# Column groups of TensorE for the sum over keys and for three conditioning vectors

## The chip, the cores and the metric

The kernel runs on one core of a Trainium2 chip. The metric is the device time of the whole program in microseconds (us), lower is better. Before the change it was 969.02 us, the median of three runs that lay between 968.61 and 970.26.

The core has five engines that run their own instruction streams and wait for each other through semaphores. PE (TensorE) multiplies matrices: it takes a stationary operand (loaded by a separate record, PEld) and streams a moving one through it into PSUM. DVE (VectorE) and ACT (ScalarE) do elementwise work, POOL (GpSimd) issues the indirect transfers here, SP issues nearly all others.

## The reference

One transformer block on X of shape (4, 512, 512), with a conditioning vector c of shape (4, 512). All is float32. Cut to what matters:

```python
mod = (silu(c) @ wmod).reshape(4, 6, 1, 512)          # six conditioning vectors per batch
sa, ca, ga, sb, cb, gb = mod[:, 0], ..., mod[:, 5]
ga, gb = away_from_zero(ga), away_from_zero(gb)       # sign * max(|.|, 0.25)
h = layernorm(x) * (1 + ca) + sa
# linear attention
Q, K, V = split(h @ W_in.T + b_in)
Q, K = rope(Q), rope(K)
A = sum over the 512 keys of (K / |K|) * V            # one row of 512 per batch
x = x + ga * ((A * Q) @ W_out.T + b_out + h)
# mixture of experts: 64 experts, 8 per token, and a shared one
h = layernorm(x) * (1 + cb) + sb
x = x + gb * moe(h)
```

The sum A is the operation in question. Per batch it is a product of a vector of 512 weights (1/|K| of each key) with a matrix of 512 keys by 512 features (K * V).

## The kernel before, in words

Tokens lie on the 128 partitions. A batch is 512 tokens, so it has TPB = 4 tiles of 128, and a row of 512 features has KC = 4 chunks of 128. The front part of the program (up to about 370 us of the profile) computes attention, the gate scores and the shared expert, batch by batch; then tiles of tokens, sorted by expert, go through the 64 experts (L1656 to L1676), and at the end the eight results of each token are read back and added.

The order is written out by hand, engine by engine. On PE (function under `@block.tensor`, from L1380) a batch goes: keys and values for each tile (`keys_values`, L1434), queries (`queries`, L1445) with the sum over keys between the second and third chunk (`sum_keys`, L1456) and `turn_sums` (L1468) behind the third, then `project` (L1479). For batch 0 the sum stands between the third and the fourth chunk of queries. Within `sum_keys` four products follow each other, one per tile of 128 keys: stationary is one column of `krn` (128 keys x 1), moving the tile of `kv` (128 keys x 512 features), and all four add into one row of PSUM bank 7. DVE copies this row into `arow` (`take_sums`, L1002), and `turn_sums` turns it into four columns with four products of one partition by 128 against a 1 (`ones1`). DVE then takes the columns (L1011) and weighs W_out with them (`weigh_w_out`, L1015), for which `project` waits.

The conditioning vectors come from `modulate(m)` (L1391): four products each, stationary four columns of silu(c), moving 128 x 512 of `wmod`, into a bank of its own. Vectors 0 to 2 are made at the start, 3 to 5 behind the keys and values of batch 0. DVE takes vectors 3 to 5 in `away_from_zero(5, ...)` (L933 to L937) and L1204, L1205, and then signals `s_modr`; PE waits for it ahead of the sum of batch 0 (the bank of vector 4 is the one the sum writes). DVE does this behind the key work, `residual(0)` and `stats1(1)`.

Each product in float32 is two records of PE in the trace, each with its own load of the stationary operand: four products are "x8", the twelve of vectors 3 to 5 "x24".

POOL scatters the places of the chosen tokens into a table (L583, 32 transfers per batch), starting when DVE has the places of a batch (L1025), and later gathers tokens (L621) for the expert phase.

Of the kernel before, what the change touches and what calls it, by code (L numbers as in the profile page):

```python
# [27 lines left out]
P = 128  # L28
BATCH = 4
SEQ = 512  # L30
D = 512
# [58 lines left out]
def build(nc, x_in, w_in, b_col, b_row, w_out, b_out, gates, experts, c_t, w_mod, tables, rope_rows,  # L90
# [8 lines left out]
    with ctx:  # L99
# [42 lines left out]
        ones_bf = sb("ones_bf", [P, P], BF16)  # L142
        ones1 = sb("ones1", [P, 1])
        tbl = sb("tbl", [P, DUMMY_COL + 1], I32)
        pair = sb("pair", [P, TILES, TOPK], I32)
# [40 lines left out]
        place = [sb(f"place{i}", [P, TPB, TOPK], I32) for i in range(2)]  # L186
        arow = region[5][0:1, 0:D]
        count_f = sb("count_f", [EV, 1])
# [40 lines left out]
        sum_bank = [bank[i] for i in (0, 1, 2, 3, 6)]  # L229
        mod_bank = [bank[m][0:BATCH, :] for m in (0, 1, 4, 6, 7, 0)]  # L230

# [25 lines left out]
        s_silu = sem("s_silu")  # L257
        s_mod = sem("s_mod")
        s_modv = sem("s_modv")
        s_modT = sem("s_modT")  # L260
# [598 lines left out]
        def _(ve):  # L859
# [5 lines left out]
            ve.memset(ones_bf[:, :], 1.0).then_inc(s_cst, 1)  # L865
            ve.memset(ones1[:, :], 1.0).then_inc(s_cst, 1)
            ve.memset(mask[:, :, 0:1], 1.0).then_inc(s_cst, 1)
            ve.memset(seen[:, TPB, :], 0.0).then_inc(s_cst, 1)
# [60 lines left out]
            def away_from_zero(m, to):  # L929

                g = mod_bank[m]
                ve.wait_ge(s_mod, m + 1)
                t0.mark(ve.tensor_scalar(mod_t[0], g, 0.0, 2.0, ALU.is_ge, ALU.mult))  # L933
                step(t0, ve.tensor_scalar(mod_t[2], g, -1.0, 0.25, ALU.mult, ALU.max))
                step(t0, ve.tensor_tensor(mod_t[1], g, mod_t[2], ALU.max))
                step(t0, ve.tensor_scalar(mod_t[2], mod_t[0], -1.0, None, ALU.add))
                step(t0, ve.tensor_tensor(to, mod_t[2], mod_t[1], ALU.mult))  # L937
# [33 lines left out]
            def key_roots(b):  # L971
# [3 lines left out]
                if b:  # L975
                    ve.wait_ge(s_rn, b)
                    ve.wait_ge(s_ar, b)
                one_over_root(t, 2, krn[:, :], s_rn)
# [18 lines left out]
            def take_sums(b):  # L997

                ve.wait_ge(s_ar, b + 1)
                if b:  # L1000
                    ve.wait_ge(s_as, b)
                ve.tensor_copy(arow[:, :], bank[7][0:1, :]).then_inc(s_arow, 1)  # L1002

# [198 lines left out]
            stats1(1)  # L1202
            away_from_zero(5, modr[1][:, 2, :])
            t0.mark(ve.tensor_scalar(modr[1][:, 0, :], mod_bank[4], 1.0, None, ALU.add))  # L1204
            step(t0, ve.tensor_copy(modr[1][:, 1, :], mod_bank[3]))  # L1205
# [175 lines left out]
        def _(pe):  # L1381
# [3 lines left out]
            def modulate(m):  # L1385
# [7 lines left out]
                mm.then_inc(s_mod, 1)  # L1393

            modulate(0)
            modulate(1)
# [52 lines left out]
            def sum_keys(b):  # L1449
# [5 lines left out]
                for i in range(TPB):  # L1455
                    mm = pe.matmul(bank[7][0:1, :], krn[:, i:i + 1], kv[:, i, :], start=(i == 0), stop=(i == TPB - 1))  # L1456
                mm.then_inc(s_ar, 1)

            def turn_sums(b):

                pe.wait_ge(s_arow, b + 1)
                pe.wait_ge(s_cst, 2)
                if b:
# [3 lines left out]
                for c in range(KC):  # L1467
                    mm = pe.matmul(bank[6][:, c:c + 1], arow[:, c * P:(c + 1) * P], ones1[0:1, :], start=True, stop=True)  # L1468
                mm.then_inc(s_as, 1)
# [109 lines left out]
            keys_values(0, *[(i, j) for i in range(TPB) for j in range(2)][1:])  # L1579
            for m in range(3, NMOD):  # L1580
                modulate(m)
            pe.wait_ge(s_modr, 1)
# [13 lines left out]
            pe.wait_ge(s_late, 16 * 4)  # L1596
            pe.wait_ge(s_cst, 5)
            for b in range(BATCH):
# [201 lines left out]
```

## Time and profile before

| | |
|---|---|
| time, median of 3 | 969.02 us (968.61 to 970.26) |
| span of the profiled execution | 1061.7 us |
| PE busy in it | 944.7 us (89%) |
| DVE busy | 547.2 us (52%) |
| POOL busy | 479.2 us (45%) |
| mean granted clock of PE | 0.960 |

The profile is one execution, and its span is the only time shown for it: it is 92.7 us above the median of the timed runs. The granted clock is a share of the full 2.4 GHz; in the windows of the trace it is 1.00 or 0.50, and values between are stretches with both.

In the rows below, a timeline line reads: start in us, busy us, engine, source line, operation, what is written and read, shape, how many, and in brackets the idle time of the engine before it with what ended it. A "x8" line merges eight records that follow each other; the last record of a group overlaps the next group's start. Chain lines read: start, us, what.

### The profile page before, as it was taken

The numbers are of one execution on the slowest core, as the hardware profiler recorded it, in microseconds if no ns is written. First come the engines' busy times: TensorE is split into PE (matmuls) and PEld (weight loads), VectorE is DVE, ScalarE is ACT, GpSimd is POOL, SyncE is SP. The second block draws the span as 40 slices with busy tenths as digits, with TensorE's granted clock in tenths as the row PEclk, the third lists the DMA queues.
The fourth block names the chain that finished last, engine by engine and source line by source line (L and its number), as shares of the span: only waits on it lengthen the run. The fifth ranks groups of instructions, "written<-read, shape, count | busy, mean of one in ns | idle before, by whom it ended". The sixth has DMA issues, their size and how long they took to land.

```text
span 1061.7 us, 18602 instructions
## 1 busy us (share of the span) xinstructions
PE 944.7 (89%) x3569; PEld 571.9 (54%) x3570; DVE 547.2 (52%) x1460; ACT 263.6 (25%) x789; POOL 479.2 (45%) x468
## 2 busy tenths in 40 slices
PE   7999999999995688989998889989898999887697
PEld 2434544544534246766766666667575666665243
DVE  4676776687685443433433334343434334343888
ACT  2122222222212103323323323233332233232000
POOL 0000066045266664555565555556565655555500
PEclk9999999999996898999999999999999999999699
DMA  9922021003021424666566666666567665797697
GB/s 345 330 69 75 1 67 28 40 1 95 0 62 43 136 80 148 222 201 216 199 193 208 241 225 212 229 199 227 197 222 227 207 213 196 250 403 263 230 420 312
DMA packets 68518, 192.06 MB, mean 181 GB/s; under 512 B 19926, under 2 KB 20438, under 8 KB 68104
## 3 DMA queue, kind: packets, MB, share of 16 engines
q1 hardware_dynamic: 38232, 120.28, 32.6%
q0 software_dynamic: 30256, 71.43, 20.5%
q8 instruction: 12, 0.20, 0.1%
q14 instruction: 18, 0.15, 0.0%
HBM read 158.98 MB, written 52.54 MB: 199 GB/s over the span
## 4 chain that ended last, share of the span: by engine, by line
PE 66%; another core or an unknown queue 8%; issue 7%; DVE 5%; DMA 4%; DVEq 1%; ACT 1%; ACTq 1%; POOLq 0%; POOL 0%; SPq 0%
PE bank L1661 19%; PE bank L1669 11%; PE bank L1434 7%; PE bank L1656 6%; PE bank L1479 5%; PE bank L1730 4%; PE bank L1445 4%; PE bank L1543 3%; PE bank L1676 2%; DMA front<-y_rows 2%; PE bank L1562 2%; DMA front<-h_rows,gid 1%; DVE front L1297 1%; PE bank L1456 1%
## 5 line engine op out<-in xcount | busy, mean ns | idle before, releaser
L1661 PE MATMUL bank<-wqkv,h2T 128*128 x1280 | 310.7, 387 | 0.0
L631 POOL DMA_INDIRECT y_rows<-front,sid x160 | 164.7, 1030 | 202.7 <-issue 90.7
L1661 PEld LDWEIGHTS bank<-wqkv,h2T 128*128 128x128 f32 x1280 | 236.6, 195 | 26.7
L583 POOL DMA_INDIRECT slot_table<-pair,place x128 | 131.1, 1024 | 249.6 <-DVE place L1025 186.5
L621 POOL DMA_INDIRECT front<-h_rows,gid x167 | 172.1, 1030 | 68.5 <-issue 46.0
L1311 DVE COPY front<-bank 128x128 f32<-128x128 f32 x160 | 46.6, 291 | 268.4 <-remote 154.4
L1669 PE MATMUL bank<-wqkv,front 128*128 x320 | 171.3, 618 | 1.3 <-DVE front L1311 1.3
L817 ACT ACTIVATE h2T<-bank 128x512 f32<-128x512 f32 x162 | 96.5, 596 | 245.8 <-PE bank L1656 145.4
L1656 PEld LDWEIGHTS bank<-const,front 128*128 128x128 f32 x648 | 82.1, 144 | 100.4 <-issue 97.2
L1305 DVE COPY front<-bank 128x512 f32<-128x512 f32 x160 | 110.0, 688 | 40.7 <-PE bank L1669 28.8
L1434 PE MATMUL bank<-wqkv,front 128*128 128x512 f32 x256 | 117.3, 610 | 8.3 <-DVEq L957 6.2
L1656 PE MATMUL bank<-const,front 128*128 128x128 f32 x648 | 100.7, 280 | 11.4 <-DMA front<-h_rows,gid 5.8
L1676 PE MATMUL bank<-const,front 128*128 128x128 f32 x160 | 45.7, 286 | 51.4 <-DVE front L1297 51.2
L1434 PEld LDWEIGHTS bank<-wqkv,front 128*128 128x128 f32 x256 | 48.5, 195 | 67.7 <-issue 58.8
L823 ACT ACTIVATE front<-bank 128x128 f32<-128x128 f32 x160 | 43.6, 272 | 98.8 <-PE bank L1661 76.3
L1297 DVE SCALAR_TENSOR_TENSOR front<-bank,wgt,front 128x128 f32<-128x128 f32 x160 | 56.0, 350 | 19.9 <-ACT front L823 16.4
L1479 PE MATMUL bank<-front 128*128 128x512 f32 x128 | 58.4, 609 | 2.9 <-DVE front L1015 2.1
L1676 PEld LDWEIGHTS bank<-const,front 128*128 128x128 f32 x160 | 22.7, 142 | 68.9 <-DVE front L1297 49.3
L1445 PE MATMUL bank<-front,wqkv 128*128 128x512 f32 x128 | 57.6, 599 | 0.0
L1669 PEld LDWEIGHTS bank<-wqkv,front 128*128 128x128 f32 x320 | 48.7, 192 | 14.7 <-issue 3.8
L1730 PE MATMUL bank<-front,const 128*128 128x512 f32 x92 | 45.1, 641 | 9.3 <-DMA front<-y_rows 9.3
L832 ACT ACTIVATE wgt<-front 128x1 f32 x160 | 32.5, 203 | 72.3 <-issue 45.4
(247 smaller groups left out, 775.2 us busy)
## 6 DMA issues: line engine op xcount, KB each, us to landing
wqkv<-in_experts SPq DMA_DIRECT2D x64, 768.0 KB
front<-y_rows SPq DMA_DIRECT2D x20, 768.0 KB, 9.3
wqkv<-y_rows SPq DMA_DIRECT2D x12, 768.0 KB, 11.7
front<-in_w_mod SPq DMA_DIRECT2D x5, 1024.0 KB, 10.5
x<-in_x SPq DMA_DIRECT2D x4, 1024.0 KB, 11.2
h_rows<-h SPq DMA_DIRECT2D x4, 1024.0 KB
out_dram<-x SPq DMA_DIRECT2D x16, 256.0 KB, 7.8
wqkv<-in_w_in SPq DMA_DIRECT2D x3, 1024.0 KB, 13.6
```

Of the source, the lines that this page charges most:

```text
L583: pool.indirect_dma_start(out=slots[:, :], out_offset=bass.IndirectOffsetOnAxis(ap=place[b % 2][:, i, k:k + 1], axis=0), in_=pair[:, b * T ...
L621: pool.indirect_dma_start(out=xg[s], out_offset=None, in_=h2_rows[:, :], in_offset=bass.IndirectOffsetOnAxis(ap=gid[:, s:s + 1], axis=0), ...
L631: pool.indirect_dma_start(out=y_rows[:, :], out_offset=bass.IndirectOffsetOnAxis(ap=sid[:, s:s + 1], axis=0), in_=yb[s % YBUFS], in_offset ...
L817: sc.activation(h2T[:, s % 4, :], bank[s % 2][:, :], ACT.Copy).then_inc(s_xT, 1)
L1305: ve.tensor_copy(yb[s % YBUFS], bank[4 + s % 2][:, :]).then_inc(s_y, 1)
L1434: mm = pe.matmul(bank[2 + j][:, :], hT[:, k, i * P:(i + 1) * P], win[:, k, (j + 1) * D:(j + 2) * D], start=(k == 0), stop=(k == KC - 1))
L1445: mm = pe.matmul(bank[4 + c % 2][:, :], win[:, k, c * P:(c + 1) * P], hT[:, k, :], start=(k == 0), stop=(k == KC - 1))
L1479: mm = pe.matmul(bank[4 + i % 2][:, :], qT[:, k, i * P:(i + 1) * P], woa[:, k, :], start=(k == 0), stop=(k == KC - 1))
L1656: mm = pe.transpose(bank[s % 2][:, k * P:(k + 1) * P], xg[s][:, k * P:(k + 1) * P], ident)
L1661: mm = pe.matmul(bank[2 + s % 2][:, 0:GU], xT[s % 4][:, k, :], wqkv[:, bass.ds(w + k * GU, GU)], start=(k == 0), stop=(k == KC - 1))
L1669: pe.matmul(bank[4 + s % 2][:, :], iT[s % 2], wqkv[:, bass.ds(w + KC * GU, D)], start=True, stop=True).then_inc(s_d, 1)
L1676: pe.transpose(bank[6 + s % 2][:, 0:P], inter[s % 2], ident).then_inc(s_I, 1)
```

## The change

The four products of the sum go to four different groups of 32 columns of the array (`tile_position=(0, 32 i)`), each with the column of `krn` repeated 32 times, so that each writes 32 equal rows of bank 7; none adds to another. DVE copies all 128 rows. `turn_sums` now multiplies the 128 partitions with a vector `heads` that is 1 at partitions 0, 32, 64 and 96 and 0 elsewhere, which adds the four partial sums. `heads` is made by five small memsets on DVE at the start. `s_ar` counts four per batch.

Vectors 3 to 5 are written to three column groups of bank 6 (partitions 64, 32 and 0), and the loops are exchanged: for each of the four chunks the three vectors follow each other. PE waits for all three pieces of `wmod` ahead of the first product, and DVE waits for all three vectors. Line numbers after the change are some 20 higher: L1456 becomes L1478, L1468 L1491, L1391 of vectors 3 to 5 L1411.

```diff
-        arow = region[5][0:1, 0:D]
+        arow = region[5][:, 0:D]
...
+        QUAD = P // TPB
+        mod_bank = [bank[m][0:BATCH, :] for m in (0, 1, 4)] + [bank[6][q * QUAD:q * QUAD + BATCH, :] for q in (2, 1, 0)]
...
+            step(t0, ve.memset(heads[:, :], 0.0))
+            for i in range(TPB):
+                ve.memset(heads[i * QUAD:i * QUAD + 1, :], 1.0).then_inc(s_cst, 1)
...
-                ve.tensor_copy(arow[:, :], bank[7][0:1, :]).then_inc(s_arow, 1)
+                ve.tensor_copy(arow[:, :], bank[7][:, :]).then_inc(s_arow, 1)
...
+            def modulate_side_by_side(ms):
+                for m in ms:
+                    pe.wait_ge(s_wmod[m], 16)
+                for k in range(KC):
+                    for m in ms:
+                        q = (NMOD - 1 - m) * QUAD
+                        mm = pe.matmul(mod_bank[m], silu_c[:, k * BATCH:(k + 1) * BATCH], wmod[m][:, k, :],
+                                       start=(k == 0), stop=(k == KC - 1), tile_position=(0, q))
+                        if k == KC - 1:
+                            mm.then_inc(s_mod_late, 1)
...
                 for i in range(TPB):
-                    mm = pe.matmul(bank[7][0:1, :], krn[:, i:i + 1], kv[:, i, :], start=(i == 0), stop=(i == TPB - 1))
-                mm.then_inc(s_ar, 1)
+                    at = slice(i * QUAD, (i + 1) * QUAD)
+                    mm = pe.matmul(bank[7][at, :], krn[:, i:i + 1].to_broadcast([P, QUAD]), kv[:, i, :], start=True, stop=True,
+                                   tile_position=(0, i * QUAD))
+                    mm.then_inc(s_ar, 1)
...
-                    mm = pe.matmul(bank[6][:, c:c + 1], arow[:, c * P:(c + 1) * P], ones1[0:1, :], start=True, stop=True)
+                    mm = pe.matmul(bank[6][:, c:c + 1], arow[:, c * P:(c + 1) * P], heads[:, :], start=True, stop=True)
```

On PE, batch 0, from vector 3 to `turn_sums`, the kernel before has this order, with the semaphores each instruction waits for (`front` holds `wmod`, `kv`, `hT` and `arow`):

```order
32 L1391 MATMUL bank<-front,silu_c 4x512 [waits s_wmod3]
33 L1391 MATMUL bank<-front,silu_c 4x512 x3
34 L1391 MATMUL bank<-front,silu_c 4x512 [waits s_wmod4]
35 L1391 MATMUL bank<-front,silu_c 4x512 x3
36 L1391 MATMUL bank<-front,silu_c 4x512 [waits s_wmod5]
37 L1391 MATMUL bank<-front,silu_c 4x512 x3
38 L1445 MATMUL bank<-front,wqkv 128x512 [waits s_win_q,s_modr]
```

The changed kernel at the same place:

```order
32 L1411 MATMUL bank<-front,silu_c 4x512 [waits s_wmod5,s_wmod4,s_wmod3]
33 L1411 MATMUL bank<-front,silu_c 4x512 x11
34 L1466 MATMUL bank<-front,wqkv 128x512 [waits s_win_q,s_modr]
35 L1466 MATMUL bank<-front,wqkv 128x512 x7
36 L1466 MATMUL bank<-front,wqkv 128x512 [waits s_qT]
37 L1466 MATMUL bank<-front,wqkv 128x512 x3
38 L1478 MATMUL bank<-front,krn 32x512 [waits s_kvp,s_rn,s_modr]
39 L1478 MATMUL bank<-front,krn 32x512 x3
```

There are still twelve products for the vectors and four for the sum, at the same places among the others; only the order among the twelve and the three waits have moved. The wait for `s_modr` ahead of the sum stands where it stood.

## Rows read from the trace of the kernel before

**Rows 1.** The page: shares of the chain that ended last, by engine.

```profile
PE 66%; another core or an unknown queue 8%; issue 7%; DVE 5%; DMA 4%; DVEq 1%; ACT 1%; ACTq 1%; POOLq 0%; POOL 0%; SPq 0%
```

**Rows 2.** The timeline of PE, batch 0, from vector 3 to the first projection.

```profile
49.69 10.46 PE L1391 MATMUL bank<-front,silu_c 128*4 128x512 f32 x24
60.08 10.57 PE L1445 MATMUL bank<-front,wqkv 128*128 128x512 f32 x24
70.58 3.59 PE L1456 MATMUL bank<-front,krn 128*1 128x512 f32 x8
74.10 3.70 PE L1445 MATMUL bank<-front,wqkv 128*128 128x512 f32 x8
...
78.26 1.03 PE L1468 MATMUL bank<-ones,front 1*128 1x1 f32 x8
...
82.41 5.37 PE L1479 MATMUL bank<-front 128*128 128x512 f32 x8 [2.10 <-DVE front L1015]
```

**Rows 3.** Line L1456 (ns min/median/max), and the groups of 0 to 345 us (L1445: busy us, mean ns).

```profile
L1456 PEld LDWEIGHTS bank<-front,krn x32: 79/84/84, 70.6 to 299.6; 128*1 128x1 f32 x32
L1456 PE MATMUL bank<-front,krn x32: 590/592/592, 70.6 to 300.0; 128*1 128x512 f32 x32
...
L1445 PEld LDWEIGHTS bank<-front,wqkv 128*128 128x128 f32 x128 | 23.7, 190 | 31.1 <-issue 31.1
```

**Rows 4.** The timeline of DVE in the same stretch of batch 0.

```profile
69.23 0.67 DVE L1205 COPY h2T<-bank 4x512 f32<-4x512 f32 x1
...
73.38 0.69 DVE L994 TENSOR_TENSOR front<-front 128x512 f32<-128x512 f32 x1
74.21 0.68 DVE L1002 COPY front<-bank 1x512 f32<-1x512 f32 x1
...
79.32 0.16 DVE L1011 COPY asum<-bank 128x4 f32<-128x4 f32 x1 [0.70 <-PE bank L1468]
```

**Rows 5.** Windows: stretch, busy us (and count) per engine, clock, DMA share, GB/s.

```profile
49.69:60.10 10.41, 10.41 (x26) 2.02 (x25) 9.23 (x23) 0.00 (x0) 0.00 (x0) 1.00 0.35 128
60.10:70.58 10.48, 10.48 (x26) 4.46 (x25) 9.65 (x30) 1.37 (x2) 0.00 (x0) 1.00 0.00 0
```

**Rows 6.** The loads of `wmod`: the timeline of SP, and line L402.

```profile
33.58 2.72 SPq L402 DMA_DIRECT2D front<-in_w_mod  x3
...
DMA to landing us min/median/max: 8.0/10.5/14.5
```

**Rows 7.** The chain that ended last, the sums of batches 1 and 3.

```profile
141.36 3.52 PE bank L1456 x8
...
297.05 3.52 PE bank L1456 x8
```

**Rows 8.** The timeline of DVE and PE in batch 1.

```profile
145.99 0.67 DVE L1002 COPY front<-bank 1x512 f32<-1x512 f32 x1
...
148.45 1.05 PE L1468 MATMUL bank<-ones,front 1*128 1x1 f32 x8
```

**Rows 9.** Windows behind three waits of PE, columns as in rows 5.

```profile
82.41:85.90 3.49, 3.49 (x5) 1.42 (x6) 0.00 (x0) 0.00 (x0) 0.00 (x0) 0.51 0.74 205
...
370.10:376.00 5.90, 5.86 (x10) 2.20 (x11) 2.24 (x9) 0.60 (x1) 0.78 (x1) 0.50 0.42 137
...
344.00:348.70 4.70, 4.70 (x9) 2.09 (x10) 4.06 (x14) 2.44 (x6) 3.48 (x5) 0.50 0.04 6
```

**Rows 10.** The timeline of PE behind another wait, and behind a long one.

```profile
127.04 3.70 PE L1434 MATMUL bank<-wqkv,front 128*128 128x512 f32 x8 [2.16 <-DVEq L957]
...
344.00 0.21 PE L1573 MATMUL bank<-mask,tri_bf 128*128 128x65 bf16 x1 [5.76 <-issue]
```

**Rows 11.** The timeline of POOL, first and last scatter of one unbroken row.

```profile
290.30 0.97 POOL L583 DMA_INDIRECT slot_table<-pair,place  x1 [19.38 <-DVE place L1025]
...
366.62 0.96 POOL L583 DMA_INDIRECT slot_table<-pair,place  x1 [0.30 <-issue]
```

**Rows 12.** The waits, 300 to 400 us: who waited for whom, us, times, longest.

```profile
DVE cum L1268 <- remote: 11.8, 1, 11.8
```

More of the change, by code:

```diff
@@ L143, in build @@
         ones1 = sb("ones1", [P, 1])
+        heads = sb("heads", [P, 1])
         tbl = sb("tbl", [P, DUMMY_COL + 1], I32)
@@ L229, in build @@
         sum_bank = [bank[i] for i in (0, 1, 2, 3, 6)]
-        mod_bank = [bank[m][0:BATCH, :] for m in (0, 1, 4, 6, 7, 0)]
+        QUAD = P // TPB
+        mod_bank = [bank[m][0:BATCH, :] for m in (0, 1, 4)] + [bank[6][q * QUAD:q * QUAD + BATCH, :] for q in (2, 1, 0)]
         s_const = sem("s_const")
@@ L258, in build @@
         s_mod = sem("s_mod")
+        s_mod_late = sem("s_mod_late")
         s_modv = sem("s_modv")
@@ L931, in away_from_zero @@
                 g = mod_bank[m]
-                ve.wait_ge(s_mod, m + 1)
+                if m >= 3:
+                    ve.wait_ge(s_mod_late, 3)
+                else:
+                    ve.wait_ge(s_mod, m + 1)
                 t0.mark(ve.tensor_scalar(mod_t[0], g, 0.0, 2.0, ALU.is_ge, ALU.mult))
@@ L976, in key_roots @@
                     ve.wait_ge(s_rn, b)
-                    ve.wait_ge(s_ar, b)
+                    ve.wait_ge(s_ar, TPB * b)
                 one_over_root(t, 2, krn[:, :], s_rn)
@@ L997, in take_sums @@
             def take_sums(b):
-                ve.wait_ge(s_ar, b + 1)
+                ve.wait_ge(s_ar, TPB * (b + 1))
                 if b:
                     ve.wait_ge(s_as, b)
-                ve.tensor_copy(arow[:, :], bank[7][0:1, :]).then_inc(s_arow, 1)
+                ve.tensor_copy(arow[:, :], bank[7][:, :]).then_inc(s_arow, 1)
             def weigh_w_out(b):
@@ L1203, in _ @@
             away_from_zero(5, modr[1][:, 2, :])
+            ve.wait_ge(s_mod_late, 3)
             t0.mark(ve.tensor_scalar(modr[1][:, 0, :], mod_bank[4], 1.0, None, ALU.add))
@@ L1455, in sum_keys @@
                 for i in range(TPB):
-                    mm = pe.matmul(bank[7][0:1, :], krn[:, i:i + 1], kv[:, i, :], start=(i == 0), stop=(i == TPB - 1))
-                mm.then_inc(s_ar, 1)
+                    at = slice(i * QUAD, (i + 1) * QUAD)
+                    mm = pe.matmul(bank[7][at, :], krn[:, i:i + 1].to_broadcast([P, QUAD]), kv[:, i, :], start=True, stop=True,
+                                   tile_position=(0, i * QUAD))
+                    mm.then_inc(s_ar, 1)
             def turn_sums(b):
                 pe.wait_ge(s_arow, b + 1)
-                pe.wait_ge(s_cst, 2)
+                pe.wait_ge(s_cst, 2 + TPB)
                 if b:
@@ L1579, in _ @@
             keys_values(0, *[(i, j) for i in range(TPB) for j in range(2)][1:])
-            for m in range(3, NMOD):
-                modulate(m)
+            modulate_side_by_side(range(3, NMOD))
             pe.wait_ge(s_modr, 1)
@@ L1596, in _ @@
             pe.wait_ge(s_late, 16 * 4)
-            pe.wait_ge(s_cst, 5)
+            pe.wait_ge(s_cst, 5 + TPB)
             for b in range(BATCH):
```

## The prediction

> **What bounds the kernel now.** I read the page first, then the chain, then the timelines of PE and DVE around each sum, then the windows for the clock. PE carries 66% of the chain [rows 1]; in the front part the sums of batches 1 to 3 stand on the chain, each with 3.52 us [rows 7]. So PE time removed there is at first sight time removed from the kernel. Batch 0 is different. PE makes vectors 3 to 5 from 49.69, the queries from 60.08, and starts the sum at 70.58 [rows 2]. The sum must wait for DVE's signal behind L1205, which ends at 69.23 + 0.67 = 69.90 [rows 4]. DVE is busy 9.23 of the 10.41 us and 9.65 of the 10.48 us ahead of it [rows 5], with work (keys, residual, statistics) that doesn't need vectors 3 to 5 until its very end. So PE has only about 0.5 us of slack there: DVE bounds that place nearly as much as PE does.
>
> The profiled span is 1061.7 us and the median 969.02, a gap of 92.7 us. The chain holds 8% (some 85 us) of "another core or an unknown queue", on a program with one core [rows 1]. My estimate is that these pauses come with being profiled. The changed places lie early, where the rows show none, so I take the differences worked out inside the profile one for one off 969.02.
>
> **The products themselves.** Thirty-two records for sixteen products: each product is two passes, 0.592 us long each, but one starts every 3.52 / 8 = 0.44 us [rows 2, 3, 7]. A product's two passes use the same columns, so they can't lie on top of each other. If PE starts its records in program order, the first pass of the next product starts only when the second pass of this one has started. Then what overlaps is always a second pass with the next product's first. Four products take 5 steps in place of 8: 5 x 0.43 + 0.08 = 2.2 us, against 3.52. The twelve products of the vectors take 13 steps in place of 24, 5.6 us in place of 10.3, a saving of 4.7.
>
> No row shows a column group, so the crossing into and out of the groups is bounded. Below: nothing, since records of different shapes already follow each other unbroken, the sum ends 3.52 us after its start and the queries start at 74.10 [rows 2]. Above: the array empties twice, 2 x (0.592 - 0.43) = 0.32 us, and one small weight load of 0.08 and one of 0.19 are uncovered [rows 3]: 0.6 us. I take 0.3, the middle. By the Trainium skill (TensorEngine Tiling (Array Packing), Key Properties) a change of tiling mode drains TensorE, which speaks against the change; by it the sum would be nearer to the upper end, about 1 us less gain over the four sums.
>
> So a sum gains 3.52 - 2.2 - 0.3 = 1.0 us.
>
> **Batch 0.** The vectors are made 4.7 - 0.3 = 4.4 us earlier and the queries with them, but then PE reaches the sum at about 66 and waits for DVE until about 70.0, with the sum, the last queries and `turn_sums` queued behind. Of the 4.4 us, 0.5 is gain. If the cover were gone, all 4.4 would count. The wait for all three loads at once costs nothing: issued by 33.58 + 2.72 = 36.3, they land at most 14.5 us later [rows 6], by about 50.8, and the queries queued behind would at most start a microsecond later: up to 4 us of delay would hide in the new wait. With the sum's 1.0 batch 0 stands at 1.5.
>
> The new wait of about 4 us has a price: the clock. Behind the 2.10 us wait at 82.41 PE ran at 0.51 for 3.49 us, 1.2 in place of 2.4 GHz, and eight records took 5.37 us [rows 2, 9]; behind one of 5.76 us it was at 0.50 for 4.70 us, and in another place for 5.90 us [rows 9, 10]. Behind a wait of 2.16 us nothing fell (3.70 us for eight) [rows 10]. A wait of 4 us I take to be long enough; the loss is then half the stretch, 1.7 us for the shortest row (up to 2.9 for the longest), and the work from 70.0 to `turn_sums` is all on the path, because DVE waits 0.70 us for `turn_sums` ahead of L1011 [rows 4]. On the other hand the 1.7 us lost at 82.41 was luck of place, as the pair of rows shows, and I give 4 in 10 that it doesn't come again: 0.7 back. Batch 0 in sum: 1.5 - 1.7 + 0.7 = 0.5 us.
>
> **Batches 1 and 2.** PE comes from work without a wait into the sum and goes on with queries. `turn_sums` needs `arow`, and DVE copies it at 145.99 to 146.66, directly behind its rotation of the queries, not because it waits for the sum [rows 8]. `turn_sums` starts at 148.45: 1.7 us is the most that any faster sum can give there. 1.0 is below it. Two batches: 2.0 us.
>
> **Batch 3.** The same 1.0 us on PE. But POOL scatters without a real pause from 290.30 to 367.6, and this row starts from the places of batch 2, ahead of the sum at 297.05 [rows 7, 11]. In the profile DVE comes later still, at 368.9, after 11.8 us in one of those foreign pauses [rows 12]; if unprofiled runs lack it, POOL is what the gathers wait for, and batch 3's gain vanishes. I count half, 0.5 us.
>
> **The rest.** Five memsets on DVE at the start lie under its wait for x; the copy of 128 rows in place of one takes the time of other 128 x 512 operations, 0.69 against 0.67 to 0.68 [rows 4]. `turn_sums` reads 128 partitions in place of one; bounds: 1.03 us for its eight records now, at most 8 x 0.02 more; nothing taken. The loads of 32 columns in place of one lie under the passes.
>
> Sum: 0.5 + 2.0 + 0.5 = 3.0 us, so 969.0 - 3.0 = **966.0 us**. Its own range, with the crossing at 0 to 0.6, the clock loss in batch 0 at 0 to 2.9 and batch 3 at 0 to 1.3, is 963.8 to 968.5.
>
> **Rival 1: all four groups run at once.** Then a sum takes two passes, 0.9 us, and with the crossing 1.2: a gain of 2.3, capped at 1.7 in batches 1 to 3 by DVE's copy. Batch 0: 0.5 + 2.3 - 1.7 + 0.7 = 1.8. With half of batch 3: 1.8 + 3.4 + 0.85 = 6.0, so 963.0 us. For it: nothing in the rows forbids a queue that holds the second passes back and lets later first passes go. Against it: the even spacing of 0.44 us that two passes of one product show. The Trainium skill (TensorE: Matmul & The Clock Gate, Part 3: Packing small matmuls) reports three column groups at 2.38 times the speed, for single-pass products, and says that matmuls start and end strictly in program order. By its ratio alone this rival would be right; by its ordering, my forecast is. Chance 0.22.
>
> **Rival 2, slower: no overlap, and the crossing is paid.** If two float32 passes in different column groups don't run together, every sum keeps its 3.5 us and gets 0.6 on top: 4 x 0.6 = 2.4 us, plus 0.1 where the vectors' own 0.6 exceeds the slack of 0.5 in batch 0: 971.5 us. It decides from 0.5 us per crossing on, where four of them pass 0.2%. For it: the trace has no pair of PE records that overlap by more than the 0.16 us of an ending pass. Against: the groups write different partitions and hold different weights. Chance 0.15.
>
> **Rival 3: the gain is given back.** Sums shorter by 1.0 us, but the clock in batch 0 stays low for 4.7 to 5.9 us as in the longer rows, the fall at 82.41 comes too, and batch 3 is swallowed: 1.5 - 2.6 + 2.0 = 0.9 us, 968.1 us. Chance 0.13.
>
> **How the numbers follow.** My forecast has the remaining 0.50. About 0.2% (1.9 us) is what a measurement of this kernel tells from no change, so faster means below 967.1 and slower above 971.0. Faster: 0.7 of my case, nearly all of rival 1: 0.35 + 0.21 = 0.56. Slower: most of rival 2 and a remnant of mine, 0.14. The rest, 0.30, is no change. The range reaches from rival 1 with a smaller crossing (961.8) to the lower part of rival 2 (970.8).
>
> **What the profile after would show.** L1478 "x8" spanning 2.2 to 2.5 us in batches 1 to 3 with starts in overlapping pairs (my case), about 1.0 to 1.2 (rival 1), or 3.6 and more (rival 2). L1411 "x24" at about 6 us, then a wait of about 4 us ahead of L1478 that ends with DVE's L1205 counterpart at about 70, and a clock of 0.5 behind it. `turn_sums` of batch 1 about 1 us nearer to the end of DVE's copy. I would be wrong if the new wait left the clock at 1.00, if the crossings were over 1 us, or if the later waits of about 2 us, whose clock falls in one place and not in another, all changed sides together: four of them at 1.7 us each weigh more than the change.

## The result and the profile after

The changed kernel takes 968.75 us (median of 20 runs, 964.20 to 971.22). The kernel before, in 20 runs beside it, takes 972.10 (968.61 to 974.26). The ratio is 0.9971, with a 95% interval of 0.9961 to 0.9982: faster by 0.29%, some 2.8 us. (The two medians differ by 3.35 us.) The forecast was 3.0 us less than before. Its time, 966.0 us, lies 2.75 us below the measured one: the three runs that it started from (median 969.02) were low ones of their kind, and 20 runs have 972.10.

The difference came out near the forecast, but not by its reasons: that it is near is luck. The sums became faster than forecast by more than a factor of two, falls of the clock took much of that back, and the two errors nearly cancel.

Shares of the chain that ended last, from the page of the kernel after:

```profile
PE 64%; DMA 9%; POOL 6%; DVE 5%; issue 5%; SPq 1%; DVEq 1%; ACT 0%; POOLq 0%
```

The entry for another core or an unknown queue [rows 1] is gone, and the span is 966.1 us against 968.06 timed for the same execution. POOL has come in with 6%: the row of scatters.

PE in batch 0, after:

```profile
50.93 3.61 PE L1411 MATMUL bank<-front,silu_c 128*4 128x512 f32 x24
54.47 10.57 PE L1466 MATMUL bank<-front,wqkv 128*128 128x512 f32 x24
71.19 1.93 PE L1478 MATMUL bank<-front,krn 128*32 128x512 f32 x8 [6.16 <-DVEq L1216]
73.06 4.32 PE L1466 MATMUL bank<-front,wqkv 128*128 128x512 f32 x8
...
77.90 1.05 PE L1491 MATMUL bank<-heads,front 128*128 128x1 f32 x8
...
82.07 6.61 PE L1502 MATMUL bank<-front 128*128 128x512 f32 x8 [2.19 <-DVE front L1024]
```

Against [rows 2]: the vectors take 54.47 - 50.93 = 3.54 us in place of 10.39. PE then stands for 6.16 us, until DVE has taken the vectors, and the sum behind this wait takes 1.87 us, as much as two passes at half clock. The eight records behind the next wait take 6.61 us, not 5.37.

The last of the vectors on DVE, and its copy of the sum:

```profile
70.40 0.69 DVE L1215 COPY h2T<-bank 4x512 f32<-4x512 f32 x1
...
75.28 0.69 DVE L1011 COPY front<-bank 128x512 f32<-128x512 f32 x1
```

It ends at 71.09, within 0.1 us of PE's restart: DVE decides that start. The copy of 128 rows takes what the one of a single row took [rows 4].

Windows behind the two waits (us, busy time and count of PE, PEld, DVE, ACT and POOL, granted clock, DMA share, GB/s):

```profile
71.00:74.50 3.50, 3.31 (x10) 1.03 (x11) 3.22 (x6) 0.00 (x0) 0.00 (x0) 0.52 0.09 22
82.00:88.00 6.00, 5.93 (x7) 2.52 (x8) 0.00 (x0) 0.00 (x0) 0.00 (x0) 0.50 0.79 279
```

The granted clock is half, 1.2 GHz in place of 2.4. Before, PE ran through the first place without a wait, and the second stretch was shorter [rows 9].

The sum of batch 1, and how its passes lie, in the timeline and in two windows that cut it at the middle:

```profile
143.91 1.06 PE L1478 MATMUL bank<-front,krn 128*32 128x512 f32 x8
144.91 0.70 PE L1466 MATMUL bank<-front,wqkv 128*128 128x512 f32 x1
```

```profile
143.91:144.34 0.43, 0.43 (x5) 0.15 (x8) 0.14 (x1) 0.32 (x1) 0.27 (x1) 1.00 0.00 0
144.34:144.91 0.57, 0.57 (x9) 0.01 (x1) 0.17 (x1) 0.36 (x1) 0.57 (x1) 1.00 0.04 1
```

The sum takes 144.91 - 143.91 = 1.00 us; before it was 3.52 [rows 7]. In the first window PE has five records: the end of a query's, and four of the sum. So four passes run at once, and the other four begin about 0.45 us after the first; the second window counts all eight and the next query.

What ends the way to `turn_sums` there now, from the chain (start, us, what):

```profile
144.02 0.70 ACT front L722
...
144.74 0.69 DVE front L996
145.43 0.65 DVE front L997
...
148.73 0.61 DVE front L1011
...
149.38 1.05 PE bank L1491 x8
```

The sum has left the chain. ACT's turn of the queries and DVE's rotation stand in its place, and PE waits for the copy in each of the batches 1 to 3:

```profile
149.38 1.05 PE L1491 MATMUL bank<-heads,front 128*128 128x1 f32 x8 [0.78 <-DVE front L1011]
...
232.06 1.05 PE L1491 MATMUL bank<-heads,front 128*128 128x1 f32 x8 [0.75 <-DVE front L1011]
...
299.65 1.05 PE L1491 MATMUL bank<-heads,front 128*128 128x1 f32 x8 [0.76 <-DVE front L1011]
```

POOL, first scatter from the places of batch 2, last scatter ahead of the gathers, first gather:

```profile
287.52 0.96 POOL L586 DMA_INDIRECT slot_table<-pair,place  x1 [18.84 <-DVE place L1034]
...
364.04 0.97 POOL L586 DMA_INDIRECT slot_table<-pair,place  x1 [0.30 <-issue]
365.31 1.05 POOL L624 DMA_INDIRECT front<-h_rows,gid  x1 [0.30 <-issue]
```

The gather follows the scatters without a pause, so POOL ends the front part. The longer idle times in this row (6.04 us once, 1.46 us three times) end with transfers of its own table, none with PE or DVE: what batch 3 gains in its sum lies beside it. From the first gather to the end it is 600.8 us here.

### The profile page after: what moved, and what is told of

It is laid out like the page before. It is cut to its first block, busy times and chain, and to the rows that moved or that the text cites. A ratio compares the mean times of both kernels' runs of the same rounds, so it can differ in the third digit from the quotient of the medians.

```text
span 966.1 us, 18609 instructions
## 1 busy us (share of the span) xinstructions
PE 902.5 (93%) x3569; PEld 560.6 (58%) x3570; DVE 553.5 (57%) x1465; ACT 271.1 (28%) x789; POOL 478.2 (49%) x468
## 4 chain that ended last, share of the span: by engine, by line
PE 64%; DMA 9%; POOL 6%; DVE 5%; issue 5%; SPq 1%; DVEq 1%; ACT 0%; POOLq 0%
PE bank L1683 25%; PE bank L1691 13%; PE bank L1455 7%; PE bank L1678 6%; POOL slot_table L586 5%; PE bank L1502 5%; DMA wqkv<-in_experts 3%; PE bank L1752 3%; PE bank L1466 2%; PE bank L1698 2%; DMA front<-y_rows 1%; DMA wqkv<-y_rows 1%; DMA front<-h_rows,gid 1%; DMA slot_table<-pair,place 1%; PE bank L1566 1%
## 5 line engine op out<-in xcount | busy, mean ns | idle before, releaser
L1683 PE MATMUL bank<-wqkv,h2T 128*128 x1280 | 303.1, 380 | 0.3 <-DMA wqkv<-in_experts 0.3
L1683 PEld LDWEIGHTS bank<-wqkv,h2T 128*128 128x128 f32 x1280 | 230.7, 190 | 25.4 <-issue 0.6
L1691 PE MATMUL bank<-wqkv,front 128*128 x320 | 164.2, 595 | 1.6 <-DVE front L1321 1.5
L1678 PEld LDWEIGHTS bank<-const,front 128*128 128x128 f32 x648 | 80.3, 141 | 92.9 <-issue 83.1
L1678 PE MATMUL bank<-const,front 128*128 128x128 f32 x648 | 97.5, 273 | 7.3 <-DMA front<-h_rows,gid 6.5
L1198 DVE TENSOR_SCALAR gid<-tbl 128x1 int32 x167 | 25.7, 154 | 82.3 <-issue 69.0
L1752 PE MATMUL bank<-front,const 128*128 128x512 f32 x92 | 43.1, 618 | 10.0 <-DMA front<-y_rows 10.0
L1698 PE MATMUL bank<-const,front 128*128 128x128 f32 x160 | 43.7, 273 | 1.0 <-issue 0.8
```

Source lines behind the costliest of these rows:

```text
L1678: mm = pe.transpose(bank[s % 2][:, k * P:(k + 1) * P], xg[s][:, k * P:(k + 1) * P], ident)
L1683: mm = pe.matmul(bank[2 + s % 2][:, 0:GU], xT[s % 4][:, k, :], wqkv[:, bass.ds(w + k * GU, GU)], start=(k == 0), stop=(k == KC - 1))
L1691: pe.matmul(bank[4 + s % 2][:, :], iT[s % 2], wqkv[:, bass.ds(w + KC * GU, D)], start=True, stop=True).then_inc(s_d, 1)
L1752: return pe.matmul(sum_bank[g % BACK][:, :], ident, back[g % BACK][k], start=(k == BY_PE - 1), stop=(k == BY_PE - 2))
```

## The experiments

All ratios are to the kernel before, measured along with each, with 95% intervals; a single execution has none. The code below is cut to what matters. A profile is one execution; its starts in us also hold what differs by chance ahead of the place: the vectors of batch 0 start between 49.56 and 51.34 us in these profiles. So stretches are compared, not starts.

**The sums alone, the vectors alone.** `sums_only` gives vectors 3 to 5 banks 6, 7 and 0 of their own, one after the other; `vectors_only` has the sum of before.

```
# sums_only, to the changed kernel
-            modulate_side_by_side(range(3, NMOD))
+            for m in range(3, NMOD):
+                modulate(m)
# vectors_only, to the changed kernel
-                    mm = pe.matmul(bank[7][at, :], krn[:, i:i + 1].to_broadcast([P, QUAD]), kv[:, i, :], ...)
+                    mm = pe.matmul(bank[7][0:1, :], krn[:, i:i + 1], kv[:, i, :], start=(i == 0), stop=(i == TPB - 1))
```

> The change with vectors 3 to 5 made as before, one after the other; only the sums over keys are in column groups. Theory A (the gain is the shorter sums of batches 1 and 2, capped at about 1.7 us each by DVE's copy; the vectors only lengthen a wait for DVE in batch 0): as fast as the whole change or a little faster, 0.25 to 0.45% below the kernel before (2.5 to 4.5 us), no wait of PE ahead of the sum of batch 0, clock 1.00 there, and the whole 2.5 us of that sum may show in batch 0. Theory B (the vectors in groups carry part of the gain, and the shorter sums are mostly hidden by the copy): less than half of the change's 2.8 us.

> The change with the sums over keys as before, four products that add into one row; only vectors 3 to 5 are in column groups. Theory A: no gain; PE waits some 6 us for DVE ahead of the sum of batch 0, the clock falls there, and the time is 0 to 2.5 us above the kernel before (0 to 0.25% slower). Theory B: 1.5 us or more faster.

Measured: `sums_only` 964.11 us, 0.9913 (0.9890 to 0.9937). `vectors_only` 971.00 us, 0.9997 (0.9978 to 1.0016). The sums alone gain three times what the whole change gains. That is more than the expectation's 0.25 to 0.45%, so its theory A was right in kind and too small. The vectors alone gain nothing, though PE spends 6.85 us less on them. PE of `sums_only`:

```profile
72.18 1.06 PE L1474 MATMUL bank<-front,krn 128*32 128x512 f32 x8
...
81.56 5.37 PE L1498 MATMUL bank<-front 128*128 128x512 f32 x8 [2.19 <-DVE front L1021]
...
126.18 3.70 PE L1451 MATMUL bank<-wqkv,front 128*128 128x512 f32 x8 [2.15 <-DVEq L963]
...
178.73 10.54 PE L1451 MATMUL bank<-wqkv,front 128*128 128x512 f32 x24 [2.05 <-issue]
...
207.08 5.40 PE L1451 MATMUL bank<-wqkv,front 128*128 128x512 f32 x8 [2.19 <-DVEq L963]
```

And the sum of batch 0 in `vectors_only`:

```profile
71.79 5.19 PE L1477 MATMUL bank<-front,krn 128*1 128x512 f32 x8 [6.34 <-DVEq L1216]
```

Without grouped vectors there is no wait ahead of the sum of batch 0 and no fall. With them the wait is 6.34 us, and even the old sum grows from 3.59 to 5.19 us: 1.6 us, about the size that the prediction gave to this fall.

**One group and two.** `one_group` is the kernel before with the stationary column repeated 32 times and a position in the array, so that the array goes into a group and out again but nothing can overlap. `two_groups` is `sums_only` with two groups, two products in each.

```
# one_group, to the kernel before
-                    mm = pe.matmul(bank[7][0:1, :], krn[:, i:i + 1], kv[:, i, :], start=(i == 0), stop=(i == TPB - 1))
+                    mm = pe.matmul(bank[7][0:32, :], krn[:, i:i + 1].to_broadcast([P, 32]), kv[:, i, :], start=(i == 0),
+                                   stop=(i == TPB - 1), tile_position=(0, 0))
# two_groups, to sums_only
-                    at = slice(i * QUAD, (i + 1) * QUAD)
+                    at = slice(i % 2 * QUAD, (i % 2 + 1) * QUAD)
```

> The kernel before with each sum's four products in 32 columns of one column group (group 0), adding into it: what it costs to enter and leave a group, with nothing overlapped. Forecast's middle: a sum of batches 1 to 3 takes 3.52 + 0.3 = 3.8 us from its first record to the next queries. Upper bound of the forecast: 4.1 us. If, as the change's own sums suggest (1.00 us for two passes of 0.43), crossing costs about nothing: 3.5 to 3.6 us, and the same time as the kernel before.

> As sums_only, but in two column groups: products 0 and 2 add into group 0, products 1 and 3 into group 1, in the order 0, 1, 2, 3. If all passes that go to different groups run together: two rounds of two passes, 2 x 0.87 = 1.8 us per sum. If only neighbouring passes of two products overlap in program order: 5 steps, 2.2 us. If a group can take a further product's passes only after the whole earlier product has drained: more than 2.0 us.

Measured: `one_group` 972.18 us, 0.9998 (0.9977 to 1.0019). `two_groups` 966.81 us in one execution. Batch 1 in `one_group`, then in `two_groups`:

```profile
144.00 3.62 PE L1456 MATMUL bank<-front,krn 128*32 128x512 f32 x8
147.55 1.98 PE L1445 MATMUL bank<-front,wqkv 128*128 128x512 f32 x4
```

```profile
142.45 1.91 PE L1474 MATMUL bank<-front,krn 128*32 128x512 f32 x8
144.29 3.70 PE L1462 MATMUL bank<-front,wqkv 128*128 128x512 f32 x8
```

The crossing is 147.55 - 144.00 - 3.52 = 0.03 us. Two groups take 144.29 - 142.45 = 1.84 us, four take 1.00: the passes of a round run at once, each round is 0.43 to 0.44 us, and 0.1 us is left over. In one group the eight passes stay 0.44 us apart, so passes of one group don't run together; the four at once in the kernel after must then be one of each product. This settles the mechanism of rival 1 and excludes pairs in a row, by which two groups and four alike would have taken 2.2 us. The prediction drew on the Trainium skill (TensorEngine Tiling (Array Packing), Key Properties), by which a change of mode drains TensorE; if so, the drain costs no more here than these 0.03 us.

**Filling the wait.** `filler` is the changed kernel with six products of known size ahead of the wait in batch 0; their result is overwritten unread.

```
+            pe.wait_ge(s_kvr, 2 * TPB)
+            for i in range(6):
+                pe.matmul(bank[2][:, :], hT[:, i % KC, 0:P], win[:, i % KC, D:2 * D], start=True, stop=True)
```

> The whole change, with six further products (128 x 128 by 128 x 512, results unused, to a free bank) on PE in its 6.2 us wait ahead of the sum of batch 0. They need 6 x 0.86 = 5.2 us, so they add nothing to the path. Theory C (what the change gives away against the version with grouped sums alone is the granted clock that falls in the new wait, with its followers): the clock stays at 1.00 through the sum of batch 0, mean clock over the runs back to about 0.978, and the time 2 to 5 us below the whole change, 0.5 to 0.8% below the kernel before. Rival D (the loss is in the grouped vectors themselves, their bank, or the wait for three loads): the time stays at 0.3% below the kernel before.

Measured: 966.52 us, 0.9952 (0.9934 to 0.9971). Its PE:

```profile
69.94 1.06 PE L1478 MATMUL bank<-front,krn 128*32 128x512 f32 x8
...
79.32 6.65 PE L1502 MATMUL bank<-front 128*128 128x512 f32 x8 [2.19 <-DVE front L1024]
```

The sum of batch 0 runs at full clock, but the work behind the next wait loses it all the same, here 6.65 us for eight records. The gain over the changed kernel is 0.19%, and the intervals overlap; the expectation was 0.5 to 0.8% below the kernel before and a clock of 0.978, and the runs show 0.48% and 0.975. The trace gives the gain a place: the sum of batch 0 to the next wait takes 79.32 - 69.94 = 9.38 us against 10.88, and every later stretch is that of the changed kernel within 0.1 us. So filling this wait returns the 1.5 us lost directly behind it and nothing of what is lost at the shorter waits.

**Moving the wait's cause.** `vectors_first` lets DVE take vectors 3 to 5 ahead of the residual and the statistics. `best` does this too and also copies the sum ahead of the rotation of the queries. `sums_copy_first` is `sums_only` with that copy ahead.

```
# vectors_first, in DVE's order
             key_roots(0)
-            residual(0)
-            ve.wait_ge(s_x1, 16)
-            stats1(1)
             away_from_zero(5, modr[1][:, 2, :])
...
             ve.nop().then_inc(s_modr, 1)
+            residual(0)
+            ve.wait_ge(s_x1, 16)
+            stats1(1)
# best and sums_copy_first, besides
-                    rope_queries(b + 1)
                     take_sums(b + 1)
+                    rope_queries(b + 1)
```

> The whole change, with DVE taking vectors 3 to 5 and signalling PE ahead of the residual and the statistics, instead of behind them. PE no longer waits ahead of the sum of batch 0. But DVE's copy of the sum stays behind all its other work, at about 75 us, so PE waits some 6 us there instead, ahead of turn_sums. Theory C: nothing or less than 2 us gained against the whole change (0.2 to 0.5% below the kernel before), because the wait and the fall of the clock only move. Rival D' (the wait ahead of the sum itself costs): 0.6% or more below the kernel before.

> As vectors_first, and DVE copies the sum of batch 0 right behind the residual, and the sums of batches 1 to 3 ahead of the rotation of the queries. Theory C with the cap by DVE's copy: batch 0's projection starts 2 to 3 us earlier than in the whole change, turn_sums of batches 1 and 2 loses its 0.75 us wait each; PE's wait in batch 0 stays below 3 us if DVE's weighing comes early enough. 0.7 to 1.2% below the kernel before. If the copy placed first makes DVE wait for the sum and so delays the rotation: batches 1 to 3 lose what they gain, 0.3 to 0.7%.

> Grouped sums alone (vectors as before), and DVE copies the sums of batches 1 to 3 ahead of the rotation of the queries. Cap by the copy: the 0.75 us waits of turn_sums vanish, 1.5 us (batches 1 and 2; that of batch 3 is ahead of POOL's row of scatters and gives nothing) below the version with grouped sums alone: about 1.0% below the kernel before. If the cap isn't real: 0.87%, no change against it.

Measured: `vectors_first` 966.17 us, 0.9942 (0.9923 to 0.9962); `best` 964.17 us, 0.9917 (0.9894 to 0.9940); `sums_copy_first` 965.05 us, 0.9921 (0.9900 to 0.9943). A row each of `vectors_first` and of `best`:

```profile
76.34 1.87 PE L1491 MATMUL bank<-heads,front 128*128 128x1 f32 x8 [5.87 <-DVE front L1011]
```

```profile
74.96 1.97 PE L1444 MATMUL bank<-const,xn 128*128 128x128 f32 x8 [5.10 <-DVE secondc L1221]
```

DVE has the same work in both, so the wait only moves: to `turn_sums`, then to the products behind it, 5.87 and 5.10 us long, and the half clock moves with it (eight records in 1.87 us against 1.05, and in 1.97 against 1.07). `vectors_first`, at 0.58% below the kernel before, lies between its two expectations (0.2 to 0.5%, and 0.6% or more) and decides nothing. `best` is faster than the changed kernel beyond the intervals: from the start of the vectors its first `project` comes after 28.33 us in place of 31.14, and its batch 1 is 1.1 us shorter.

`sums_copy_first` was expected at about 1.0% below the kernel before and has 0.79%; `sums_only` has 0.87%. Its wait for the copy is gone in all batches, and from the wait in batch 1 (125.95, clock fallen) to the one in batch 2 it needs 53.25 us, where `sums_only` (clock not fallen) needs 52.55: without the 1.7 us of the fall that is 1.0 us less. In batch 2 the copy, now placed first, makes DVE wait 0.61 us for the sum, and the weighing of W_out comes later:

```profile
80.05 6.63 PE L1498 MATMUL bank<-front 128*128 128x512 f32 x8 [2.19 <-DVE front L1021]
...
234.92 3.67 PE L1498 MATMUL bank<-front 128*128 128x512 f32 x8 [1.51 <-DVE front L1021]
```

There this wait takes the place of the one removed, and the stretch is 0.4 us longer. The time is that of `sums_only` within the intervals. The first row matters for all that follows: up to here `sums_copy_first` has the code of `sums_only`, and the same eight records take 6.63 us against 5.37. How long such a fall lasts varies between executions of the same work.

**The wait without the grouping.** `short_vectors` is `sums_only` with the vectors computed as before, one after the other, but only four of their twelve products: the rest of vectors 3 to 5 is left out, so that PE comes to the wait as early as in the changed kernel.

```
-                modulate(m)
+                ks = (0, 1) if m == 3 else (0,)
+                for k in ks:
+                    mm = pe.matmul(mod_bank[m], silu_c[:, k * BATCH:(k + 1) * BATCH], wmod[m][:, k, :], ...)
```

> Grouped sums alone, and vectors 3 to 5 not in column groups but cut short: four products in place of twelve (chunks 0 and 1 of vector 3, chunk 0 of vectors 4 and 5), 3.4 us as long as the grouped ones; the rest of these vectors is left out. PE gets the same wait of 6 us ahead of the sum of batch 0 as in the whole change, without any grouped vector. Theory C (the wait and the clock behind it are what costs): about the time of the whole change, 0.1 to 0.5% below the kernel before, mean clock of the runs 0.970 to 0.974. Rival D (the column groups of the vectors, their shared bank or the common wait cost): about the time of grouped sums alone, 0.87% below.

Measured: 969.01 us, 0.9979 (0.9964 to 0.9995), as its theory C expected, beside 0.9971 for the changed kernel and 0.9913 with all twelve. **Eight products fewer make the kernel slower:** by 4.9 us by the medians (964.11 to 969.01), each measured beside its own runs of the kernel before (972.18 and 972.08).

```profile
71.09 1.93 PE L1474 MATMUL bank<-front,krn 128*32 128x512 f32 x8 [6.22 <-DVEq L1212]
...
82.03 6.64 PE L1498 MATMUL bank<-front 128*128 128x512 f32 x8 [2.19 <-DVE front L1021]
```

The rows are those of the changed kernel within 0.1 us, and from the start of the sum of batch 0 to the first scatter of batch 2's places it is 216.32 us here, 216.33 in the changed kernel and 211.73 in `sums_only`. So the loss is not the column groups of the vectors and not their joint wait for the loads; it comes with PE arriving early. One reserve: the cut vectors change what the gate sees, so tokens may go to other experts. From the first gather to the end this profile has 604.0 us against 601.6 in `sums_only`; but `best`, with all vectors, has 604.2, so this alone shows nothing.

**Filling the short waits too.** `warm` is `sums_only` with products that nobody reads, against the 128 x 128 unit matrix, in the waits of about 2 us: two in batch 0 behind `turn_sums`, one or two in each later batch, and two more in batch 2. `warm_after` is the changed kernel with these and with six in the long wait.

```
+            def keep_busy(to, n):
+                for _ in range(n):
+                    pe.matmul(to, ident, win[:, 0, D:2 * D], start=True, stop=True)
...
+            pe.wait_ge(s_kvr, 2 * TPB)
+            keep_busy(bank[2][:, :], 2)
...
-                    keys_values(b + 1, (2, 1), (3, 0))
+                    keys_values(b + 1, (2, 1))
+                    pe.wait_ge(s_or, TPB * (b + 1))
+                    keep_busy(bank[4][:, :], 1 if b == 2 else 2)
+                    keys_values(b + 1, (3, 0))
```

> Grouped sums alone, with one or two further products (0.86 us each, results unused) in each of the waits of 1.5 to 2.2 us that PE has ahead of the projection of batch 0, ahead of the last tiles' keys of batches 1 to 3 and ahead of the keys of batch 2. They add nothing to the path. Theory C: the falls of the clock between 70 and 300 us are gone (two such falls in the version with grouped sums alone), 1.7 us each: 1.1 to 1.4% below the kernel before, mean clock 0.981 or more. If the falls come whatever PE does in these waits: 0.87%, clock 0.978.

> The whole change, with the six products in the long wait of batch 0 and the same further products in the shorter waits as in warm. Theory C (the clock is all that the whole change loses against grouped sums alone): the same time as warm within 0.2%. Rival D: it stays 0.3% or more behind warm.

Measured: `warm` 959.38 us, 0.9872 (0.9847 to 0.9897); `warm_after` 960.62 us, 0.9890 (0.9865 to 0.9915). Both beat both kernels. PE of `warm`:

```profile
78.36 1.88 PE L1468 MATMUL bank<-wqkv,const 128*128 128x512 f32 x4
80.71 3.67 PE L1502 MATMUL bank<-front 128*128 128x512 f32 x8 [0.47 <-DVE front L1021]
...
123.74 3.67 PE L1451 MATMUL bank<-wqkv,front 128*128 128x512 f32 x8 [0.54 <-DVEq L963]
...
204.72 3.67 PE L1451 MATMUL bank<-wqkv,front 128*128 128x512 f32 x8 [0.57 <-DVEq L963]
```

The expectation of `warm` was 1.1 to 1.4% and is met with 1.28%; so is that of `warm_after`. Behind each filled wait eight records take 3.67 us, where they took 5.37 to 6.65 when the clock fell, and 3.70 when it held. The same stretch, 0 to 130 us, in the kernel after, in `sums_only`, in `short_vectors` and in `warm_after`:

```profile
0.00:130.00 130.00, 112.00 (x340) 49.44 (x342) 82.63 (x229) 28.82 (x50) 1.64 (x7) 0.94 0.48 168
```

```profile
0.00:130.00 130.00, 117.67 (x353) 50.55 (x354) 83.34 (x230) 28.90 (x51) 1.64 (x7) 0.99 0.48 168
```

```profile
0.00:130.00 130.00, 112.00 (x324) 49.32 (x326) 82.44 (x229) 28.81 (x50) 1.64 (x7) 0.94 0.48 167
```

```profile
0.00:130.00 130.00, 120.26 (x381) 53.96 (x383) 86.41 (x242) 29.01 (x51) 1.64 (x7) 1.00 0.46 168
```

The clock is 0.94 in the two kernels that come early to the wait, 0.99 in `sums_only`, and 1.00 with the waits filled. A single profile says less here than it seems to: `sums_copy_first`, with the code of `sums_only` in this stretch, has 0.96. Over all runs the mean clock is 0.971 in the changed kernel and in `short_vectors`, 0.978 in `sums_only`, and 0.982 and 0.983 in `warm` and `warm_after`.

With the waits filled, the time with grouped vectors and with plain ones is the same within the intervals (0.9890 and 0.9872), and from the start of the sum of batch 0 to the first scatter of batch 2's places both profiles have the same length, 208.56 and 208.55 us. So most of what the whole change lost against the sums alone was clock.

**The kernel before, once more.**

> The kernel before once more, for a profile of it. If the foreign pauses of the first profile came with that one execution: a span near 970 us, POOL's first gather some 79 us behind its first scatter of batch 2, as in the changed kernel (77.8 us), with nothing of DVE in between.

Measured: 970.92 us in one execution, with a span of 969.1. As expected, the chain has no entry for another core, and the first gather follows POOL's last scatter after 0.30 us:

```profile
367.90 1.05 POOL L621 DMA_INDIRECT front<-h_rows,gid  x1 [0.30 <-issue]
```

The pauses of [rows 1, 12] were of that one execution, not of the kernel. In it the gather came at 375.22; without them POOL's row sets the end in the kernel before as well. From this gather to the end it is 969.1 - 367.9 = 601.2 us, against 600.8 after. The gain lies in the front part.

## Why the difference was near and the mechanism wrong

The profile of `before_again` has no pauses and is the base of this account. Each stretch is the difference of two starts in it and in the trace of after, as read in their timelines:

| stretch | before_again | after | difference | sums_only | difference |
|---|---|---|---|---|---|
| start of the sum, batch 0 | 71.74 | 71.19 | -0.55 | 72.18 | +0.44 |
| to the first `project` | 11.83 | 10.88 | -0.95 | 9.38 | -2.45 |
| to the wait ahead of the sum of batch 1 | 44.63 | 45.89 | +1.26 | 44.62 | 0.0 |
| to the wait in batch 2 (holds a sum) | 56.05 | 54.34 | -1.71 | 52.55 | -3.50 |
| to the next wait in batch 2 | 28.36 | 30.06 | +1.70 | 28.35 | 0.0 |
| to the wait in batch 3 (holds a sum) | 69.58 | 67.58 | -2.00 | 69.25 | -0.33 |
| to the first scatter of batch 2's places | 7.57 | 7.58 | 0.0 | 7.58 | 0.0 |
| the start of that scatter | 289.76 | 287.52 | -2.24 | 283.91 | -5.85 |

The kernel after in parts: -0.24 us up to the wait of batch 1, -1.71 and -2.00 where the sums of batches 1 and 2 lie, and +1.70 for a fall of the clock at 182.30 that `before_again` lacks. The forecast had -0.5, -1.0, -1.0 and, for batch 3, -0.5. Of `sums_only`, +0.44 in the first line only says that its vectors start at 51.29 in place of 50.85.

**The overlap: the step that failed.** "the first pass of the next product starts only when the second pass of this one has started": this made 2.2 us for a sum. All four first passes run together, then all second ones: 1.00 us with the crossing. The vectors show it too, three at a time, 3.54 us for twelve products. The Trainium skill (TensorE: Matmul & The Clock Gate, Part 3: Packing small matmuls) has matmuls start and end in program order; applied to the two passes of a float32 product, as the forecast did, this does not hold here. The ratio of 2.38 that it reports for three groups was the better guide, and 10.39 / 3.54 = 2.9 is still above it. I had put more trust in the order than in the ratio, and gave rival 1 only 0.22.

**The start of the sum, mis-sized.** The forecast time begins at 969.02 us, the median of three runs; 20 runs have 972.10. These 3.1 us are as much as the whole gain that was forecast.

**The crossing, mis-sized.** 0.3 us was taken; `one_group` shows 0.03. Nothing was taken for `turn_sums`, whose eight records take 1.05 us in place of 1.03; the bound given with it, 8 x 0.02 us, comes from no row.

**The range.** Its lower end, 961.8, is rival 1 "with a smaller crossing". But rival 1 is capped by the copy, so without any crossing it gains only 0.3 us more, in batch 0: 962.7. And with its three terms all at their best ends the forecast's own sum gives 962.6, not 963.8.

**The cap, as worked out.** A faster sum in batches 1 to 3 was said to gain at most 1.7 us, because of DVE's copy [rows 8]. Batch 1 shows -1.71, and PE now waits 0.75 to 0.78 us for the copy. The 2.52 us of a sum are 1.7 gained and 0.8 waited, as in rival 1. Batch 2 shows -2.00, 0.3 more than the cap that was read in batch 1.

**Batch 0: the slack as worked out, the price mis-sized.** Of the vectors' time 0.5 us was to be gain; it is 0.55, and by `vectors_only` the rest is hidden. The wait is 6.16 us, not 4, because the vectors take 3.54 us and not 5.6. The fall of the clock behind it was foreseen at 1.7 us; to the first `project` the changed kernel loses 10.88 - 9.38 = 1.5 us to `sums_only`, which is that. The term "I give 4 in 10 that it doesn't come again: 0.7 back" brought nothing: the fall at 82.07 came again and was longer, +1.26 us. That it was longer can't be put down to the change, since `sums_copy_first` has the longer one too (80.05 to 125.95 is 45.90 us, against 44.62 in `sums_only`). Batch 0 with that is -0.55 - 0.95 + 1.26 = -0.24 us, against -0.5 in the forecast and -1.8 in rival 1.

**Batch 3 gives nothing.** Half of its gain was counted. POOL's row begins at the places of batch 2 and has no longer wait there that ends with PE or DVE: 287.52 to 365.31 is 77.79 us, and 289.76 to 367.90 in `before_again` is 78.14.

**Where the rest went.** The sums alone gain 0.87%, the whole change 0.29%. The difference is 0.58% or 5.6 us, and by the two filled kernels most of it is clock. As a bound, from the mean granted clock of all runs, PE was at half clock for (1 - 0.971) x 2 x 966 = 56 us a run in the kernel after and for 42 us with the sums alone, 14 us more, which would cost half of that, 7 us, if all of it lay on the path. The pair of profiles differs by 4.6 us from the start of the sum of batch 0 to the scatters (216.33 and 211.73): 1.5 directly behind the new wait, 1.3 in the longer fall behind it, and 1.8 in the falls further on. Of rival 3 the mechanism was right and its size was off, because it stood beside the smaller gain. It took 2.1 us from the forecast's 3.0; rival 1's 6.0 less 2.1 is 3.9 us, against the measured 2.8.

**What stays open.** The waits of about 2 us lose the clock in one place and keep it in another, with the same lengths. PE of the kernel after, and of the second profile of the kernel before:

```profile
127.96 5.40 PE L1455 MATMUL bank<-wqkv,front 128*128 128x512 f32 x8 [2.17 <-DVEq L966]
...
182.30 12.23 PE L1455 MATMUL bank<-wqkv,front 128*128 128x512 f32 x24 [2.05 <-issue]
...
212.36 3.70 PE L1455 MATMUL bank<-wqkv,front 128*128 128x512 f32 x8 [2.20 <-DVEq L966]
```

```profile
128.20 5.40 PE L1434 MATMUL bank<-wqkv,front 128*128 128x512 f32 x8 [2.17 <-DVEq L957]
...
184.25 10.54 PE L1434 MATMUL bank<-wqkv,front 128*128 128x512 f32 x24 [2.05 <-issue]
...
212.61 3.70 PE L1434 MATMUL bank<-wqkv,front 128*128 128x512 f32 x8 [2.19 <-DVEq L957]
```

All three are the other way round in `sums_only` (126.18, 178.73 and 207.08), and the first place held the clock in the first profile of the kernel before [rows 10] and lost it in the second. So the times and mean clocks over many runs show that early arrival costs more than the 1.5 us behind the new wait, but not how: whether the later falls follow from the first is not settled. `filler`, which has no fall at the new wait, stays 0.39% behind `sums_only`, with intervals that just overlap. Nor was the kernel before tried with the filled waits alone, so `warm`'s gain is not split between them and the sums, except by `sums_only`: 0.9913 to 0.9872, each beside its own runs of the kernel before.

## What to carry to other kernels

Where small-output float32 products follow each other on the path, put them side by side in column groups: here four take 1.00 us, little more than one of them (3.52 / 4 = 0.88 us), and going in and out takes 0.03 us by `one_group`. Before PE work ahead of a wait for another engine is shortened, ask what PE does in the time that it wins: an idle PE can come back at half speed, and then less work makes the kernel slower. Where such a wait can't be avoided, products that nobody reads may be worth more than the time they take.

## What the hardware showed unexpectedly

- Passes in different column groups run at once, across the two passes of float32: 4 products in 1.00 us against 3.52, 2 groups in 1.84, 12 products in three groups in 3.54 against 10.39.
- One group in, one group out: 0.03 us.
- Leaving out eight of twelve products made the kernel 4.9 us slower by the medians (`short_vectors` against `sums_only`).
- The same work behind the same wait took 5.37 us in one execution and 6.63 in another (`sums_only`, `sums_copy_first`), by how long the clock stayed at half.
- Filling five waits, most of about 2 us, with one or two products each was worth 0.4 to 0.5% over `sums_only`, with intervals that just overlap. The five runs of the filled kernel lie within 958.26 to 960.44; the 17 of the kernel before beside it within 967.99 to 973.83.
